# Filler matmuls of TensorE: one more at each of their places, and at ten more places, at both ends of a transformer block

## What is computed

```
x = x + layernorm(attn(layernorm(x)))      # 16 heads, softmax over 256 keys, w_qkv, w_out
x = x + layernorm(moe(layernorm(x)))       # logits = x @ Wr + bias, top 2 of 8 experts, softmax of the two
moe: sum over experts rw * (silu(x Wg) * (x Wu)) Wd  +  (silu(x Sg) * (x Su)) Sd
```

## Time and profile before

| | us |
|---|---|
| median of 3 runs | 379.01 |
| lowest and highest run | 377.48, 380.12 |
| the profiled execution, whole | 380.47 |
| its span, first to last instruction | 378.7 |
| TensorE busy in it | 359.4 |
| VectorE, ScalarE, GpSimd busy | 310.7, 267.4, 200.8 |

### The profile page before, as it was taken

The page is one execution under the profiler, slowest core; times in us unless marked ns, Lnnn a source line. Parts: engine busy times, 40 slices in busy tenths (PEclk is TensorE's granted clock), DMA queues, the critical chain, the costliest instruction groups (busy, mean ns, idle before and its releaser), DMA issues.

```text
span 378.7 us, 10110 instructions
## 1 busy us (share of the span) xinstructions
PE 359.4 (95%) x3342; PEld 231.8 (61%) x3342; DVE 310.7 (82%) x788; ACT 267.4 (71%) x511; POOL 200.8 (53%) x518
## 2 busy tenths in 40 slices
PE   7898799999999999999999999999999999999992
PEld 7866556455465557575657565665665566677872
DVE  8476579989899998989998889999998896767461
ACT  4563368788977877887878877786868876964522
POOL 5723121615556374848472835674744655858644
PEclk9999899999999999999999999999999999999998
DMA  2139766847534728557616937544773042222201
GB/s 76 44 105 150 180 123 131 183 140 153 148 105 137 181 54 205 142 144 174 140 58 165 230 103 182 132 121 121 161 181 113 7 115 74 85 74 69 71 8 38
DMA packets 59922, 45.65 MB, mean 121 GB/s; under 512 B 8966, under 2 KB 56966, under 8 KB 59870
## 3 DMA queue, kind: packets, MB, share of 16 engines
q1 hardware_dynamic: 56638, 44.02, 46.5%
q10 hardware_dynamic: 3232, 0.99, 2.3%
HBM read 26.69 MB, written 17.81 MB: 118 GB/s over the span
## 4 chain that ended last, share of the span: by engine, by line
PE 61%; issue 10%; POOL 7%; DMA 6%; DVE 6%; ACT 4%; SPq 3%; ACTq 1%; POOLq 0%; DVEq 0%
PE pvp L674 13%; PE sc L643 8%; PE sc L658 8%; PE bank_d L824 7%; PE bank_d L840 6%; PE bank_d L825 5%; PE bank_d L681 3%; PE bank_a L726 3%; DVE mx L1036 3%; DMA pv_dram<-pv_sb 2%; POOL rstd L1178 2%; POOL hidden L1245 2%; PE bank_d L797 2%; PE bank_a L735 2%; DMA ks<-qk_dram 1%
## 5 line engine op out<-in xcount | busy, mean ns | idle before, releaser
L1036 DVE TENSOR_REDUCE mx<-sc 128x4 f32<-128x1024 f32 x128 | 153.9, 1220 | 20.3 <-PE sc L643 19.4
L888 ACT ACTIVATE pr<-sc 128x1024 f32<-128x1024 f32 x128 | 129.8, 1024 | 32.8 <-PE sc L658 32.3
L674 PE MATMUL pvp<-pr,va 128*32 128x256 f32 x1024 | 68.5, 385 | 0.0
L824 PE MATMUL bank_d<-x3T,wg_sb 128*128 128x256 f32 x160 | 54.8, 424 | 1.3 <-DVE hidden L1134 1.2
L658 PE MATMUL sc<-qs,ks 51*128 51x256 bf16 x512 | 48.8, 274 | 4.1 <-DMA qs<-mT 2.0
L643 PE MATMUL sc<-ks,qs 48*128 48x256 bf16 x512 | 48.9, 274 | 1.1 <-DVE mx L1036 0.7
L1173 POOL TENSOR_TENSOR vareps<-mv,eps 128x2 f32<-128x2 f32 x64 | 12.6, 197 | 67.0 <-DVE mv L1028 67.0
L825 PE MATMUL bank_d<-x3T,wu_sb 128*128 128x256 f32 x160 | 47.6, 379 | 0.0
L1245 POOL TENSOR_TENSOR hidden<-hidden,rwb 128x256 f32<-128x256 f32 x60 | 43.0, 731 | 6.6 <-DMA rwb<-rw_dram 6.3
L1178 POOL TENSOR_TENSOR rstd<-vareps,mhalf 128x2 f32<-128x2 f32 x64 | 44.5, 696 | 0.0
L971 ACT ACTIVATE th<-bank_d 128x256 f32<-128x256 f32 x80 | 30.7, 384 | 18.4 <-PE bank_d L825 16.7
(11 more groups left out here) (113 smaller groups left out, 503.9 us busy)
## 6 DMA issues: line engine op xcount, KB each, us to landing
rwb<-rw_dram SPq DMA_DIRECT2D x30, 256.0 KB, 4.3
qk_dram<-parts SPq DMA_DIRECT2D x30, 192.0 KB, 3.4
qs<-qk_dram SPq DMA_DIRECT2D x30, 192.0 KB, 4.5
ks<-qk_dram SPq DMA_DIRECT2D x30, 192.0 KB, 5.1
qk_dram<-parts SPq DMA_DIRECT2D x30, 128.0 KB, 3.0
pv_dram<-pv_sb SPq DMA_DIRECT2D x14, 256.0 KB, 2.8
x_sb<-in_L_attn_x_dram SPq DMA_DIRECT2D x16, 128.0 KB, 3.0
out_dram<-x SPq DMA_DIRECT2D x16, 128.0 KB, 1.8
```

The costliest lines, as they stand in the source:

```text
L674: mm = pe.matmul(pvp[32 * j:32 * j + 32, g, :], values[:, X * c + 4 * g + j, 32 * tt:32 * tt + 32], pr[:, k, c * N:(c + 1) * N], start=(tt ...
L824: pe.matmul(bank_d[bank][:, 0:N], wg_sb[:, ORDER[n], :], x3T[b % 2][:], start=True, stop=True)
L888: nc.scalar.activation(pr[:, 2 * s:2 * s + 2, :].rearrange("p k n -> p (k n)"), sc[PAIR["s2", b, s]][:].rearrange("p u c n -> p (u c n)"), ...
L1036: nc.vector.tensor_reduce(mx[b % 2][:, :, :, s].rearrange("p c u -> p u c"), sc[PAIR["s1", b, s]][:], AX.X, ALU.max).then_inc(max_done, 1)
```

## The change

Each place in the two tables that holds filler matmuls gets one more, except `xT` of batch 0, which stays at 24. Ten places are new with one matmul each: `s1_5`, `s2_0`, `s2_1` of batch 0, `s1_6`, `s2_3`, `s2_7` of batch 1, and at the end `down` of batch 13, `gu1` of batch 14, `gu1` and `gu4` of batch 15. `FILL` goes from 89 to 121 matmuls, `FILL_LAST` from 14 to 27. Nothing else is changed.

```diff
--- before.py
+++ after.py
@@ -239,14 +239,14 @@
 
 
 FILL = {
-    "maxT": {0: 10, 1: 1}, "proj": {0: 2}, "qk": {0: 2, 1: 2, 2: 1}, "s1_2": {1: 2, 2: 1}, "s1_3": {1: 3},
-    "s1_4": {0: 2, 1: 3}, "s1_5": {3: 1}, "s1_6": {0: 3, 3: 2}, "s1_7": {0: 3, 1: 1}, "s2_0": {1: 5},
-    "s2_1": {1: 2}, "s2_4": {0: 3, 1: 2}, "s2_5": {0: 2, 1: 2}, "sel1": {0: 3}, "v": {1: 1},
-    "xT": {0: 24, 3: 5, 4: 1},
+    "maxT": {0: 11, 1: 2}, "proj": {0: 3}, "qk": {0: 3, 1: 3, 2: 2}, "s1_2": {1: 3, 2: 2}, "s1_3": {1: 4},
+    "s1_4": {0: 3, 1: 4}, "s1_5": {0: 1, 3: 2}, "s1_6": {0: 4, 1: 1, 3: 3}, "s1_7": {0: 4, 1: 2},
+    "s2_0": {0: 1, 1: 6}, "s2_1": {0: 1, 1: 3}, "s2_3": {1: 1}, "s2_4": {0: 4, 1: 3}, "s2_5": {0: 3, 1: 3},
+    "s2_7": {1: 1}, "sel1": {0: 4}, "v": {1: 2}, "xT": {0: 24, 3: 6, 4: 2},
 }
 FILL_LAST = {
-    "down": {15: 2}, "gu0": {15: 1}, "gu2": {14: 1, 15: 1}, "gu3": {14: 1, 15: 1}, "gu4": {14: 3},
-    "router": {14: 2, 15: 2},
+    "down": {13: 1, 15: 3}, "gu0": {15: 2}, "gu1": {14: 1, 15: 1}, "gu2": {14: 2, 15: 2}, "gu3": {14: 2, 15: 2},
+    "gu4": {14: 4, 15: 1}, "router": {14: 3, 15: 3},
 }
```

## The result

The changed kernel takes 383.45 us in the median of 4 runs (383.1 to 383.8), the kernel before 379.06 (377.48 to 380.12). The ratio is 1.0125, with a 95% interval of 1.0085 to 1.0166. The profiled execution is 383.59 us with a span of 381.8, against 380.47 and 378.7.

What follows compares the result with a forecast made beforehand. The prediction took TensorE, busy 95% of the span, to bound the kernel. Its terms, 0.7 + 4.6 + 0.2 - 1.6 = 3.9 us, on the median of 379.0 gave 382.9 us, with a range of 379.6 to 385.0.

Steps and rivals of the forecast that it cites:

- One filler costs 0.22 us at an old place, 0.47 at a new one: On TensorE: one more filler where some stand costs 0.22 us, a new place between two score steps 0.47 us.
- Up to 20.9 us nothing: Start to 20.9 us: three added fillers, at `qk` and `sel1` of batch 0 and `qk` of batch 1, cost 0.
- The four ahead of `v`: 20.9 to 28.0 us: four fillers hold back `v` and ScalarE's DMA issues; 0.7 us, bounds 0 and 0.9.
- The eight at the waits: 28.0 to 41.6 us: eight fillers ahead of waits of 1.33 and 1.98 us cost nothing, up to 1.8 us without cover.
- The middle: 41.6 to 77 us: seventeen fillers on TensorE's chain, thirteen at old and four at new places, lengthen it by 4.6 us.
- The end: Thirteen fillers at the end, most ahead of waits for VectorE, cost 0.2 us in all, bounds 0 and 1.0.
- The clock: The slow stretch of 42.0 to 45.4 us goes as fillers shrink two waits: minus 1.6 us, bounds minus 1.7 and 0.
- Half given back behind 77 us: Rival: VectorE or DMAs pace stretches behind 77 us, half of the 5.5 us delay goes; 380.2 us, chance 0.18.
- The other side: Rival: filler keeps TensorE fast and costs nothing, idle time at all seventeen places of 41.6 to 77 us; 377.4 us, chance 0.10.
- short idles all along: Argument against filler paying at short idle places: despite such idles the granted clock is 1.00 from 45.4 to 340 us.
- The signs: Changed profile: L681 242 records, L685 54, no 0.5 clock at 40 to 50 us, qs<-mT wait near 1.1, `qk` 3.7 us later.
- the bounds of the parts: Front 0 to 0.9 us, middle 4.0 to 5.0, end 0 to 1.0, given as the source of the range 379.6 to 385.0.

Runs made afterwards that it cites:

- front_only: Kernel before with only the fifteen fillers that the change adds up to `s2_0` of batch 0 (41.6 us); 379.91 us, ratio 1.0036.
- front_no_mid: Kernel before with the change's fifteen added front fillers and none of its own 27 fillers between 41.6 and 77 us; 381.88 us, ratio 1.0059.
- four_only: Kernel before with only the four added fillers ahead of `v` of batch 2; 383.06 us, ratio 1.0062.
- eight_only: Kernel before with only the eight added fillers between 28.0 and 41.6 us; 378.61 us, ratio 0.9994.
- mid_only: Kernel before with only the seventeen fillers that the change adds between 41.6 and 77 us; 383.96 us, ratio 1.0145.
- mid_minus: Kernel before with one filler fewer at each of its 13 places between 41.6 and 77 us; 379.02 us, ratio 1.0000.
- before_again: The kernel before once more, unchanged; 378.64 us, ratio 1.0013.
- mid_plus2: Kernel before with two more fillers at each of 13 old places between 41.6 and 77 us and two at four new ones; 387.42 us, ratio 1.0242.
- early_v: As two_waits, with one filler fewer at each of the four places ahead of `v` of batch 2; 378.70 us, ratio 0.9990 to the kernel before.
- two_waits: Kernel before with four more fillers ahead of `maxT` of batch 0 and four ahead of `s2_0` of batch 0; 377.93 us, ratio 0.9985.
- no_fill: Kernel before with no filler but the 24 of `xT` of batch 0 at the start; 382.22 us, ratio 1.0087.

## Why the prediction was right

The forecast was 382.9 us with a range of 379.6 to 385.0; the measured median is 383.45, in the range and to the side that it named. Set against the later sessions' executions of before without a slow stretch (378.0 us), the change costs 5.4 us; the three terms of the sum apart from the clock, 0.7 + 4.6 + 0.2, make 5.5. So the number isn't luck, though one term was too large and one explanation wrong. By its own steps:

- **One filler costs 0.22 us at an old place, 0.47 at a new one.** Measured 0.22 at every old place. At the four new ones of the middle 0.42, 0.35, 0.51 and 0.35, in all 1.63 for the 1.7 that I had.
- **Up to 20.9 us nothing.** Right: the shift is -0.02 us at `qk` of batch 1.
- **The four ahead of `v`, 0.7 us.** They push `v_copy` by 0.78 and, against the execution without a slow stretch, `s2_0` by 0.92. Against the profile of before it is -0.11, since the DMA there took 1 us longer. The size holds, within what `s2_0` moves from one execution to the next: the same front gives 0.72 in front_only and 1.27 in front_no_mid. Which execution it is read against decides whether it is seen. four_only alone costs more, by the clock.
- **The eight at the waits, nothing.** Right for the delay (eight_only: 0.09 us at `s2_0`), open for the time: eight_only has 0.6 us more than the kernel before without a slow stretch.
- **The middle, 4.6 us.** 4.07 net in the traces, which is 4.46 of filler less the 0.39 that a wait for a DMA took up; mid_only 5.0 by the medians. Right as a price of what is added, wrong as an explanation: I wrote that filler there fills no idle time and holds the next step back. front_no_mid and mid_minus show that the old fillers stood in waits that are there without them. A chain that joins without a gap tells that TensorE is one of the longest paths, and not by how much the next path is shorter.
- **The end, 0.2 us.** 0.01 us in the trace.
- **The clock, minus 1.6 us.** The size is right: the steps from `s2_0` to 46.5 us, which hold 0.64 us of added filler, went by 0.82 us faster, 1.5 us for the clock. But I subtracted it from the median as if every execution of before paid it. Three of six profiled ones did, and 38 of 97 by the mean clock, which puts 0.8 us into the median. This is the term that was mis-sized. With 0.8 the sum is 4.7, 383.7 us, beside the 383.45 measured. The profiled execution of before is 1.4 us above its median, which could have told me. By the rule that it weighed, the prediction also put the bound of what the clock can give at 1% of the span, 3.8 us. The Trainium skill, TensorE: Matmul & The Clock Gate, "Part 1: The HAM clock gate", gives its under 1% for the ramp at the start, which no run here looks at. For stretches inside the launch it is no bound here: the nine executions of four_only with the long stretch are 4.4 us above the other three, by medians.
- **Half given back behind 77 us.** No: 2.89 us at 77 us, 3.13 at the end, and in between it moves by up to 0.5 us both ways. Against before_again it is 4.99 and 5.14. mid_plus2 loses 0.95 of its 3.96 us on mid_only, a quarter and not half.
- **The other side.** The fillers did cost, so it never came to its price. The "short idles all along" that the prediction held against it are thin: none between 45 and 77 us, and ten waits with 3.2 us in all from there to 340.
- **The signs.** L681 has 242 records and L685 54, and nothing runs at half clock between 40 and 50 us. The `qk` matmuls of 77.7 us came 2.9 us later and not 3.7, since in the profile of before the DMA of the maxima was itself 1 us late, and of the wait for it (qs<-mT) nothing was left where I expected 1.1. And the bounds of the parts add up to 2.3 to 7.2 us, 381.3 to 386.2, which isn't the range that the prediction says it gets from them.

What stays open: the ten executions of front_only without a slow stretch have a median of 379.9 us, 1.8 above the kernel before without one, and the four fillers ahead of `v` account for 0.7 to 0.9 of it. Behind 80 us the shifts between two executions of unlike kernels move by up to 2 us. In early_v against two_waits it goes from 0.68 to 2.48 us between 98 and 106 us, where VectorE waits 1.68 us for the DMA den<-pv_dram in early_v and not at all in two_waits. And the executions of the kernel before alone scatter over 6 us. I have no experiment that tells those apart.

## What to carry to other kernels

Filler for the clock costs the path nothing only up to the wait that it stands ahead of (`s2_0` moved by 0.09 us in eight_only, 0.15 in two_waits); in a schedule where it was fitted to the waits, one more per place is paid in full, and one fewer gains nothing. So the chain can price what is added, but to price a removal look for the next path, or take it out and look at the waits. Filler right ahead of the longest waits took the slow stretch away in all twelve executions of two_waits; four fillers on the way to them (four_only) brought one in nine of twelve. Before a gain from the clock is subtracted from a median, count in how many executions the slow stretch is there: the mean granted clock of each tells it.

## What the runs showed of the hardware

The granted clock isn't the program's alone: the same kernel had a stretch at half clock in one execution and none in another, with the DMA ahead of it landing at 41.6 us in the one and 40.6 in the other. By the mean clock at least 38 of 97 executions of that kernel had one. Each low stretch that I saw inside a launch came behind waits and lasted from 3.4 us to 20.5 (no_fill). In the three profiles of the old front with the stretch the wait for the DMA was 1.98, 1.75 and 1.36 us, in the three without it 1.00, 0.99 and 0.74. The Trainium skill, TensorE: Matmul & The Clock Gate, "Part 1: The HAM clock gate", says of the start of a kernel that the number of slow matmuls varies from run to run. No run here looks at the start; the executions here show that a slow stretch in the middle of a launch comes and goes as well. With 30.7 us at half clock the median of no_fill is only 3.4 us above that of before, net of the fillers that it doesn't have.
